# Attention row sums from a column of ones, and the fold of the values' halves on TensorE

## The reference

```python
# attention, 16 heads of 32 columns
q, k, v = split_heads(x @ Wq + bq), split_heads(x @ Wk + bk), split_heads(x @ Wv + bv)
attn = einsum('bhqd,bhkd->bhqk', q, k) / sqrt(32) + alibi      # alibi: slope of the head times distance
p = softmax(where(causal, attn, min), axis=-1)
out = einsum('bhqk,bhkd->bhqd', p, v)
x = layernorm(x + merge_heads(out) @ Wo + bo)
# feed-forward, 4 experts of width 2048, each token through its top one
probs = softmax(x @ Wr + br); top_w, top_idx = top_k(probs, 1)
y = top_w * ((silu(x @ Wg[e]) * (x @ Wu[e])) @ Wd[e])          # e = top_idx
x = layernorm(x + y)
```

## Time and profile before

| | |
|---|---|
| time, median of 3 runs | 1331.99 us (1330.33 to 1332.3) |
| profiled execution, its own time | 1333.06 us |
| its span | 1331.3 us, mean granted TensorE clock 0.945 |
| busy PE, PE weight loads, DVE, ACT, POOL | 1208.9, 1084.3, 801.7, 579.5, 309.1 us |
| HBM read and written | 64.74 MB and 9.18 MB |

### The profile page before, as it was taken

The page is one execution under the profiler, slowest core; times in us unless marked ns, Lnnn a source line. Parts: engine busy times, 40 slices in busy tenths (PEclk is TensorE's granted clock), DMA queues, the critical chain, the costliest instruction groups (busy, mean ns, idle before and its releaser), DMA issues.

```text
span 1331.3 us, 28183 instructions
## 1 busy us (share of the span) xinstructions
PE 1208.9 (91%) x8697; PEld 1084.3 (81%) x8697; DVE 801.7 (60%) x1999; ACT 579.5 (44%) x1597; POOL 309.1 (23%) x450
## 2 busy tenths in 40 slices
PE   5988998999999988559999999999999999999983
PEld 4877887888788776559989998999989998899961
DVE  4566777677666675626565546654566456554665
ACT  3667766676677675024233323332233323232310
POOL 4200200020011020351133113320233123311347
PEclk9999999999999998569999999999999999999985
DMA  8222323222322230152312322232312231222112
GB/s 248 65 53 55 71 65 96 47 68 63 96 49 60 65 104 16 64 158 64 89 57 72 88 73 76 61 88 65 96 49 80 67 95 56 72 83 79 33 41 87
DMA packets 109641, 100.15 MB, mean 75 GB/s; under 512 B 12799, under 2 KB 81791, under 8 KB 109504
## 3 DMA queue, kind: packets, MB, share of 16 engines
q1 hardware_dynamic: 106464, 89.16, 24.6%
q0 software_dynamic: 3040, 9.18, 2.2%
HBM read 64.74 MB, written 9.18 MB: 56 GB/s over the span
## 4 chain that ended last, share of the span: by engine, by line
PE 72%; POOL 7%; DVE 7%; issue 5%; ACT 5%; DMA 3%; SPq 2%; ACTq 0%; POOLq 0%; DVEq 0%
PE bank L761 33%; PE bank L552 13%; PE bank L786 9%; PE bank L676 4%; POOL up_lo L1318 4%; PE bank L661 3%; PE bank L773 2%; PE bank L650 2%; DMA up_raw<-in_Wu_dram 2%; POOL out_dram L1364 2%; ACT probs L860 2%; DVE scores L1049 1%; PE bank L685 1%; SPq L460 1%; PE bank L638 1%
## 5 line engine op out<-in xcount | busy, mean ns | idle before, releaser
L761 PE MATMUL bank<-up_hi,xsT_hi 128*128 x1216 | 357.5, 294 | 9.2 <-POOL up_lo L1318 5.8
L761 PE MATMUL bank<-up_lo,xsT_hi 128*128 x1216 | 345.0, 284 | 3.1 <-issue 3.1
L761 PE MATMUL bank<-up_hi,xsT_lo 128*128 x1216 | 345.2, 284 | 2.2 <-issue 2.2
L1318 POOL TENSOR_TENSOR up_lo<-up_raw,up_hi 128x256 fp32r<-128x256 f32 x241 | 170.0, 742 | 502.8 <-ACT up_hi L892 502.5
L1194 DVE SCALAR_TENSOR_TENSOR h_tok<-bank,row_weight,silu 128x128 f32<-128x128 f32 x304 | 93.4, 346 | 310.9 <-ACT silu L950 310.9
L761 PEld LDWEIGHTS bank<-up_hi,xsT_hi 128*128 128x128 f32 x1216 | 233.7, 192 | 17.6 <-issue 17.6
L761 PEld LDWEIGHTS bank<-up_hi,xsT_lo 128*128 128x128 f32 x1216 | 234.6, 193 | 2.0 <-issue 2.0
L761 PEld LDWEIGHTS bank<-up_lo,xsT_hi 128*128 128x128 f32 x1216 | 234.1, 192 | 2.3 <-issue 2.3
L950 ACT ACTIVATE silu<-bank 128x256 f32<-128x256 f32 (+1 forms) x160 | 59.9, 374 | 392.4 <-PE bank L761 377.8
L1211 DVE TENSOR_TENSOR y<-bank,y 128x512 f32<-128x512 f32 x304 | 204.9, 689 | 0.4
L860 ACT ACTIVATE probs<-scores,neg_max 128x512 f32<-128x512 f32 (+3 forms) x256 | 142.3, 557 | 69.1 <-DVE neg_max L1049 68.5
(11 more groups left out here) (155 smaller groups left out, 2173.2 us busy)
## 6 DMA issues: line engine op xcount, KB each, us to landing
up_raw<-in_Wg_dram SPq DMA_DIRECT2D x64, 256.0 KB, 3.1
up_raw<-in_Wu_dram SPq DMA_DIRECT2D x64, 256.0 KB, 3.8
down_raw<-in_Wd_dram SPq DMA_DIRECT2D x64, 256.0 KB, 2.7
k_stack<-qk_hi SPq DMA_DIRECT2D x128, 64.0 KB, 2.0
q_stack<-qk_hi SPq DMA_DIRECT2D x128, 64.0 KB, 2.0
x_tok<-in_x_dram SPq DMA_DIRECT2D x4, 1024.0 KB, 5.8
k_stack<-qk_lo SPq DMA_DIRECT2D x64, 64.0 KB, 2.0
q_stack<-qk_lo SPq DMA_DIRECT2D x64, 64.0 KB, 2.0
```

Source lines behind the costliest of these rows:

```text
L761: mm = pe.matmul(bank[:, n * 2 * P:(n + 1) * 2 * P], a[:, s, k, :], up_w[w][k][:, :, :].rearrange("p a f -> p (a f)")[:, bass.ds(at, 2 * P ...
L1318: pool.tensor_tensor(up_w[1][k][:, e, :], up_raw[:, idx % NUPS, k, :, :].rearrange("p g f -> p (g f)"), up_w[0][k][:, e, :].bitcast(F32), ...
```

## The change

`v` gets a 65th column to each head that holds 1.0 (POOL writes it once, in eight copies, at the start), so the product with the values has a 65th row: the sum of the probabilities, high plus low parts. ACT's exponential loses `accum_out`. In place of the four transposes of a head there are four matmuls in type fp32 (`pvT` and `fold` are fp32, not fp32r): stationary a 65x128 block of `pvT`, moving a matrix `fold` of 65 rows and 33 columns. `fold` is two 32x32 identities above each other and a single 1.0 in the corner, so that this product transposes the block, adds the two halves and carries the row sum into column 32. ACT's copy to `pv_hi` and DVE's addition go. DVE now takes the reciprocal from PSUM and itself multiplies the values out of PSUM into `o_tok`; POOL's multiply goes. PE's wait for the bank is now for `s_o` (DVE's multiply) where it was for `s_pvsum`.

```diff
+VW = 2 * HD + 1
...
-NRS = 4
...
-        v = p1.put("v", [P, 2, QT, 2 * GH, 2 * HD], F32R)
+        v = p1.put("v", [P, 2, QT, 2 * GH, VW], F32R)
...
-        pvT = p1.put("pvT", [2 * HD, SEQ], F32)
+        pvT = p1.put("pvT", [VW, SEQ], F32)
+        fold = p1.put("fold", [VW, HD + 1], F32)
...
-        pv_hi = p1.put("pv_hi", [P, 2, QT, HD], F32)
-        pv_sum = p1.put("pv_sum", [P, 2, QT, HD], F32)
...
-        row_sum = p1.put("row_sum", [P, NRS, QT], F32)
...
-        s_pv, s_pvhi, s_pvsum = semaphore("pv_done"), semaphore("pv_hi_copied"), semaphore("pv_summed")
+        s_pv, s_fold = semaphore("pv_done"), semaphore("fold_set")
+        s_vones = semaphore("ones_column_set")
...
+                if u == 0:
+                    pe.wait_ge(s_vones, 2 * QT)
+                    pe.wait_ge(s_fold, 3)
...
-                    pe.wait_ge(s_pvsum, hd - 1)
+                    pe.wait_ge(s_o, hd - 1)
...
                         for part in (pT_hi, pT_lo):
-                            mm = pe.matmul(bank[0:2 * HD, i * P:(i + 1) * P], v[:, g // 2 % 2, j, g % 2 * GH + h, :],
+                            mm = pe.matmul(bank[0:VW, i * P:(i + 1) * P], v[:, g // 2 % 2, j, g % 2 * GH + h, :],
                                            part[:, u % 2, at + j * P:at + (j + 1) * P],
...
                 bank = banks[4 + hd % 2]
...
                 for i in range(QT):
-                    mm = pe.transpose(bank[:, i * 2 * HD:(i + 1) * 2 * HD], pvT[:, i * P:(i + 1) * P],
-                                      ident[0:2 * HD, 0:2 * HD])
+                    mm = pe.matmul(bank[:, i * (HD + 1):(i + 1) * (HD + 1)], pvT[:, i * P:(i + 1) * P], fold[:, :],
+                                   start=True, stop=True)
                 mm.then_inc(s_back, 1)
...
             def unit_exp(u):
...
-                hd = g * GH + h
...
-                if u % PER_HEAD == 0 and hd >= NRS:
-                    act.wait_ge(s_inv, hd - NRS + 1)
                 for i, at, width in spans(tiles):
...
-                                        bias=neg_max[:, u % 2, i:i + 1], accum_out=row_sum[:, hd % NRS, i:i + 1])
+                                        bias=neg_max[:, u % 2, i:i + 1])
                 ex.then_inc(s_exp, 1)
...
             def unit_transposed(u):
...
                 act.wait_ge(s_pv, (hd + 1) * PER_HEAD)
...
-                act.activation(pvT[:, :], banks[4 + hd % 2][0:2 * HD, :], ACT.Copy).then_inc(s_pvT, 1)
-            def head_values(hd):
-                parts = banks[4 + hd % 2][:, 0:QT * 2 * HD].rearrange("p (i s d) -> p i s d", i=QT, s=2)
-                act.wait_ge(s_back, hd + 1)
-                if hd >= 2:
-                    act.wait_ge(s_pvsum, hd - 1)
-                act.activation(pv_hi[:, hd % 2, :, :], parts[:, :, 0, :], ACT.Copy).then_inc(s_pvhi, 1)
+                act.activation(pvT[:, :], banks[4 + hd % 2][0:VW, :], ACT.Copy).then_inc(s_pvT, 1)
...
             def split_up(c, e):
...
-                    if u >= 4 + PER_HEAD and (u - 4) % PER_HEAD == 0:
-                        head_values((u - 4) // PER_HEAD - 1)
-            head_values(NB * NH - 1)
...
             def head_values(hd):
-                parts = banks[4 + hd % 2][:, 0:QT * 2 * HD].rearrange("p (i s d) -> p i s d", i=QT, s=2)
-                dve.wait_ge(s_exp, (hd + 1) * PER_HEAD)
+                g, h = divmod(hd, GH)
+                b, m = divmod(g, GPB)
+                sums = banks[4 + hd % 2][:, 0:QT * (HD + 1)].rearrange("p (i d) -> p i d", i=QT)
+                dve.wait_ge(s_back, hd + 1)
...
-                dve.reciprocal(row_inv[:, hd % 2, :], row_sum[:, hd % NRS, :]).then_inc(s_inv, 1)
-                dve.wait_ge(s_pvhi, hd + 1)
-                dve.tensor_tensor(pv_sum[:, hd % 2, :, :], parts[:, :, 1, :], pv_hi[:, hd % 2, :, :],
-                                  ALU.add).then_inc(s_pvsum, 1)
+                dve.reciprocal(row_inv[:, hd % 2, :], sums[:, :, HD]).then_inc(s_inv, 1)
+                if hd == 0:
+                    dve.wait_ge(s_wo, 1)
+                    dve.wait_ge(s_wlo, len(W_ORDER))
+                if b >= 2 and g % GPB == 0 and h == 0:
+                    dve.wait_ge(s_side, done("OT", (b - 2) * QT + QT - 1))
+                dve.wait_ge(s_inv, hd + 1)
+                dve.tensor_tensor(o_tok[:, b % 2, :, m * P + h * HD:m * P + (h + 1) * HD], sums[:, :, 0:HD],
+                                  row_inv[:, hd % 2, :].unsqueeze(2).to_broadcast([P, QT, HD]), ALU.mult).then_inc(s_o, 1)
+            dve.wait_ge(s_set, 1)
+            dve.wait_ge(s_ident, 16)
+            for n in range(2):
+                dve.tensor_copy(fold[n * HD:(n + 1) * HD, 0:HD], ident[n * HD:(n + 1) * HD, n * HD:(n + 1) * HD]).then_inc(s_fold, 1)
+            dve.tensor_copy(fold[2 * HD:VW, HD:HD + 1], ident[2 * HD:VW, 2 * HD:VW]).then_inc(s_fold, 1)
...
         def gpsimd(pool):
...
+            pool.memset(fold[:, :], 0.0)
             pool.memset(hot_pad[:, :, :].bitcast(F32), 0.0).then_inc(s_set, 1)
+            pool.wait_ge(s_set, 1)
+            for n in range(2):
+                for j in range(QT):
+                    pool.tensor_copy(v[:, n, j, :, 2 * HD], ones[:, 0:2 * GH]).then_inc(s_vones, 1)
...
-            def head_values(hd):
-                g, h = divmod(hd, GH)
-                b, m = divmod(g, GPB)
-                if hd == 0:
-                    pool.wait_ge(s_wo, 1)
-                    pool.wait_ge(s_wlo, len(W_ORDER))
-                pool.wait_ge(s_pvsum, hd + 1)
-                if b >= 2 and g % GPB == 0 and h == 0:
-                    pool.wait_ge(s_side, done("OT", (b - 2) * QT + QT - 1))
-                pool.tensor_tensor(o_tok[:, b % 2, :, m * P + h * HD:m * P + (h + 1) * HD], pv_sum[:, hd % 2, :, :],
-                                   row_inv[:, hd % 2, :].unsqueeze(2).to_broadcast([P, QT, HD]), ALU.mult).then_inc(s_o, 1)
             def split_up(c, e):
...
-                if u >= 4 + PER_HEAD and (u - 4) % PER_HEAD == 0:
-                    head_values((u - 4) // PER_HEAD - 1)
...
-            head_values(NB * NH - 1)
...
```

## The result

The changed kernel takes 1342.03 us (median of 4 runs, 1339.81 to 1347.62) against 1331.84 for the kernel before: ratio 1.0075, 95% interval 1.005 to 1.0099. It is slower by 10 to 11 us; the forecast was 14.5 us more, a median of 1346 us. The profiled execution of the changed kernel took 1347.62 us, the longest of its four.

A forecast was written before the change was run, and what follows sets the result against it. The prediction took TensorE's order of work to bound attention. Fold +25.5, 65th column +1 and ACT's relief -12 gave +14.5 us: 1347.6 us for the profiled execution, a median of 1346; range 1317 to 1376, its own case 1335 to 1360.

The forecast's parts named there:

- TensorE bounds the stage: Attention, 50 to 525 us: TensorE's order of work sets the pace, its matmuls about two thirds of the chain.
- The fold's eight pairs: The fold on TensorE: 8 load-and-matmul pairs a head at 0.115 us, +0.50 us a head, +25.5 us in all.
- a ninth load: After the fold on TensorE: the next job's own load, charged 0.115 us beside the 8 pairs, 1.04 us together.
- 51 of the 64 heads: Heads charged for the fold: 38 on the path in full and 26 by half.
- The term: The fold's cost on TensorE's path: 51 heads at +0.50 us, +25.5 us.
- The Trainium skill's four passes: Fold: a true fp32 product takes four array passes; with no shared load, 16 pairs a head, +72 us, chance 10%.
- The 65th column: Values matmuls on TensorE: 1280 loads of 65 columns for 64, 0.8 ns each, +1 us.
- my 0.54 us for before: TensorE, kernel before: time from a head's last values matmul to the next job's first one, transposes between.
- ACT's relief: ACT in attention loses 48 us of reads and 17 us of copies, 65 of 328 busy us; gain 12 us.
- Start, end, the rest: Setup on POOL and DVE, and the chain behind the last head: 0 us; feed-forward stage as long as before.
- The first up product: Sign in the profile after: it starts about 14 us later, with the feed-forward stage as long as before.

The follow-up runs named there:

- fold_twice: The changed kernel with each of a head's four fp32 products issued twice, 16 pairs in place of 8; ratio 1.0517 to the kernel before.
- col65: The kernel before with only the 65th column of ones in the values, read by nobody, and so 65-row transposes; ratio 0.9956 to the kernel before.
- fold_fp32r: The changed kernel with pvT and fold in fp32r, four pairs a head in place of eight, low part left out; ratio 0.9881 to the kernel before.
- ones_only: The kernel before with the 65th column of ones and no accumulator reads; transposes, ACT's copy, DVE's addition and POOL's multiply stay; ratio 0.9928 to the kernel before.
- fold_transpose: The changed kernel with four 65x128 fp32 transposes a head for the fold's products, halves not added; ratio 0.9829 to the kernel before.
- dve_copy: ones_only with the copy of the high halves made by DVE in place of ACT, computation complete; ratios 0.9833 and 0.9849 to the kernel before.

## Why the prediction was right

**TensorE bounds the stage.** Right: fold_twice pays 0.112 us for each further pair.

**The fold's eight pairs.** Right in number (512 records) and nearly in price: 0.108 us in the chain against 0.115. The step from 0.54 us was to be one to 1.04 us, +0.50; the timeline shows 0.92, +0.38, and the chain +0.47 (0.39 to 0.86). About half of that difference is the pair's price; the other half is that I had charged a ninth load of 0.115 us, where the fold's first matmul starts 0.06 us after the last values matmul and the next job's load is hidden. Between 50 and 525 us, 53 folds stand in the chain of the changed kernel where I had charged 51 of the 64 heads. The term was 25.5 us; measured are 34 against transposes of 65 rows, or 28 against those of 64 rows, with the 6 us that col65 gains. Twice the loads with the same shapes (fold_fp32r to changed) are 27 us. The Trainium skill's four passes (FP8 and Floating Point Precision, TensorE Precision Notes) fit this trace only if two of them share a load: it has two load and matmul records to a product.

**The 65th column.** The load costs 1 ns more (139 to 140), as forecast. That 65 rows in `pvT` also take away gaps around the transposes was inside my 0.54 us for before, but I had not seen it as a gain of its own that the kernel could have without the fold.

**ACT's relief, forecast 12 us.** The size is about right, partly by luck, and the basis is wrong. I took the reads at 48 us by adding up their records, and 65 us with the copies, a fifth of ACT's time; what ACT got back is 34 us, a tenth, since half of each read lies under its exponential. On that basis my own estimate would have been 12 x 34/65, about 6 us, and the sum +20. What made up for it is that, without the fold, half of the 34 us reached the time, where I had assumed less than a fifth (12 of 65): from ones_only over col65 the reads give 4 us; from fold_transpose over ones_only, which drops the copy and joins DVE's and POOL's work, 13 us. Together 17, and the parts close the balance: +34 for the fold, -6 for the shape, -4, -13 make +11 us, the measured 0.0085. That sum closes by construction, since each term is a difference of neighbours; what it shows is the sizes. Beside the fold the reads are worth 1 to 3 us and the copy 6, since TensorE then leaves little to gain. I had given three quarters of the relief to the reads because of the length of their records. The copy gave at least as much, and engines waited on either side of it. That the waits and not the busy time are the cause is argued from the waits and from dve_copy, in which DVE takes on more work and the kernel still gains; the copy's wait and its 0.27 us weren't varied apart.

**Start, end, the rest.** The end of the loop moved by 9 to 12.5 us, which is the whole difference. The first up product began at 577.9 us before and at 590.1 and 587.6 us in the two executions of the changed kernel, 10 to 12 us later where I had forecast 14. From it to the last one it took 698 us before and 701 and 690 us after, within what this stage varies by itself.

## What to carry to other kernels

A narrow fp32 matmul costs here what its pairs of load and matmul cost: count them (two for a true fp32 product, one for a transpose or for fp32r), take the time of a pair from a narrow matmul of the same kind already in the trace (a transpose's pair was cheaper, 0.06 against 0.11 us), and ask whether the engine has cover there; here it had none. Moving an addition onto the engine that bounds the stage can lose even where it takes instructions off two others. Don't add up records that overlap: four reads of 0.19 us a head were 0.33 us of ACT's time, not 0.75. And look for operations that stand between two waits of other engines, not only for long ones: one 0.27 us copy was worth at least as much as the four reads.

## What the runs showed of the hardware

- An fp32 product of 65x128 by 65x33 is two loads (199 ns each on the mean) and two matmuls. Eight such pairs took 0.86 us at a granted clock of 1.00 (the fold at 308.01 us) and 1.66 us at 0.50 (the one at 75.73 us). In fp32r it is one pair, 0.10 us.
- An fp32 transpose of 64 rows by 128 columns took 0.39 us for four in the chain, one of 65 rows 0.26 to 0.27 us: one row more and a third less time, and the gaps of 0.15 us on each side of them are gone.
- ACTIVATION_READ_ACCUMULATOR has a record of 188 ns but adds about 0.08 us to ACT's busy time (21 us for 256): it starts before its exponential ends.
- The same multiply that lay in POOL's idle time cost 10 us by time, 5 by the loop's end, when it was put on DVE, though DVE was busy for only 326 of 475 us.
